# A mixture-of-experts block with attention on one core: both shared pieces of an expert period ahead of the down projection, rows turned between them, down weights split in mid-period

## What is computed

```python
x = x + 0.5 * ffn(layernorm(x));  x = x + attention(layernorm(x));  x = x + 0.5 * ffn(layernorm(x))

def ffn(inp):                                  # 4096 tokens x 256
    x = w_norm * inp * rsqrt(mean(inp**2) + 1e-6)
    w_topk, sel = top_k(softmax(x @ w_router), 4)          # 32 experts, 4 of them for a token
    buf[e] = the first 128 tokens that chose expert e      # capacity 128
    y[e] = (silu(buf[e] @ w_gate[e]) * (buf[e] @ w_up[e])) @ w_down[e]    # 256 -> 176 -> 256
    out[token] += y[e, slot] * w_topk                      # scatter-add
    shared = (silu(x @ sw_gate) * (x @ sw_up)) @ sw_down   # 256 -> 704 -> 256, for all tokens
    return inp + out + sigmoid(x @ w_shared_gate) * shared
```

## Time and profile before

| | |
|---|---|
| three runs, median (lowest to highest) | 946.34 us (943.54 to 947.62) |
| the profiled execution, its own time | 943.53 us |
| its span, first to last instruction | 941.8 us |
| TensorE busy | 899.0 us, 95% |
| VectorE busy | 731.3 us, 78% |
| ScalarE busy | 579.3 us, 62% |
| GpSimd busy | 513.9 us, 55% |
| TensorE's granted clock, mean | 0.997 |

### The profile page before, as it was taken

One profiled execution on the slowest core, in us unless ns is written; L12 is line 12 of the kernel. 1 busy time (PEld: TensorE's weight loads), 2 busy tenths in 40 slices (PEclk: granted clock), 3 DMA queues, 4 the chain that ended last, 5 costly groups with the idle time before them and its releaser, 6 DMA issues.

```text
span 941.8 us, 18520 instructions
## 1 busy us (share of the span) xinstructions
PE 899.0 (95%) x6246; PEld 688.6 (73%) x6246; DVE 731.3 (78%) x1768; ACT 579.3 (62%) x922; POOL 513.9 (55%) x537
## 2 busy tenths in 40 slices
PE   8999998999999999999999999989999989999997
PEld 6778886877878856666666666558788868778786
DVE  6998786765565889999998999988887867665545
ACT  6676744344444478878887888867667433444432
POOL 6343304456653588887887788934333045566530
PEclk9999999999999999999999999999999999999999
DMA  8143245777874610010001002004432457778735
GB/s 259 50 139 103 75 132 149 176 174 183 192 166 101 201 46 24 23 43 24 23 23 45 22 11 82 21 12 129 142 98 74 127 155 175 174 178 199 162 39 177
DMA packets 95515, 101.93 MB, mean 108 GB/s; under 512 B 18768, under 2 KB 86736, under 8 KB 95440
## 3 DMA queue, kind: packets, MB, share of 16 engines
q1 hardware_dynamic: 83152, 83.17, 29.3%
q0 software_dynamic: 12288, 17.83, 11.1%
HBM read 65.44 MB, written 35.54 MB: 107 GB/s over the span
## 4 chain that ended last, share of the span: by engine, by line
PE 52%; DVE 21%; issue 13%; POOL 6%; ACT 5%; DMA 2%; DVEq 0%; POOLq 0%; ACTq 0%
PE gu L91 6%; PE gu L93 6%; PE gu L92 6%; PE zT L1058 4%; PE pj_at L91 3%; PE pv_at L1815 3%; PE pj_at L93 3%; PE pj_at L92 3%; PE down L91 2%; PE down L93 2%; PE down L92 2%; PE scores_at L1799 2%; POOL out L841 2%; DVE turned_at L2057 2%; POOL rows L833 2%
## 5 line engine op out<-in xcount | busy, mean ns | idle before, releaser
L1144 ACT CAST a_hi<-act_gu 128x512 fp32r<-128x512 f32 x96 | 59.3, 618 | 94.6 <-DVE act_gu L1396 68.2
L91 PE MATMUL gu<-x_hi,gu_hi 128*128 128x512 f32 x264 | 113.4, 429 | 1.3 <-DVE act_gu L1396 1.2
L833 POOL DMA_INDIRECT rows<-z_rows,slots x64 | 71.1, 1110 | 67.5 <-DVE slots L1383 48.5
L1917 ACT ACTIVATE capped_at<-scores_at 128x2048 f32<-128x2048 f32 x64 | 93.1, 1454 | 20.6 <-PE scores_at L1799 20.4
L93 PE MATMUL gu<-x_lo,gu_hi 128*128 128x512 f32 x264 | 103.9, 393 | 0.0
L92 PE MATMUL gu<-x_hi,gu_lo 128*128 128x512 f32 x264 | 103.3, 391 | 0.0
L1925 ACT ACTIVATE probs_at<-capped_at 128x2048 f32<-128x2048 f32 x64 | 95.2, 1487 | 2.5
L1994 POOL TENSOR_SCALAR_AFFINE_SELECT probs_at<-probs_at 128x1024 f32<-128x1024 f32 x64 | 85.6, 1342 | 9.6 <-ACT probs_at L1925 8.8
L91 PE MATMUL down<-down_hi,a_hi 128*128 128x256 f32 x300 | 89.8, 299 | 0.6 <-DVE a_lo L1406 0.4
L1058 PE MATMUL zT<-w_gu,xT 128*128 128x352 f32 x256 | 88.4, 468 | 0.1
L841 POOL DMA_INDIRECT acc<-base,slots x32 | 51.2, 1599 | 65.2 <-DMA acc<-base,slots 53.3
(11 more groups left out here) (269 smaller groups left out, 2807.4 us busy)
## 6 DMA issues: line engine op xcount, KB each, us to landing
w_gu<-in_w_gate SPq DMA_DIRECT2D x64, 176.0 KB
w_gu<-in_w_up SPq DMA_DIRECT2D x64, 176.0 KB
w_down<-in_w_down SPq DMA_DIRECT2D x64, 176.0 KB
z_rows<-z SPq DMA_DIRECT2D x16, 512.0 KB, 3.6
acc<-base SPq DMA_DIRECT2D x10, 512.0 KB, 3.4
out<-base SPq DMA_DIRECT2D x10, 512.0 KB, 3.2
xn_at<-acc SPq DMA_DIRECT2D x16, 256.0 KB, 2.8
x<-xn_at SPq DMA_DIRECT2D x16, 256.0 KB, 2.1
```

Of the source, the lines that this page charges most:

```text
L91: nc.tensor.matmul(out, w_hi, x_hi, start=first, stop=False)
L833: pool.indirect_dma_start(out=gathered_rows[:, n, :], out_offset=None, in_=m.z_rows, in_offset=bass.IndirectOffsetOnAxis(ap=slots[:, e:e + ...
L1144: nc.scalar.copy(a_hi[rows_, mt, :], act_gu[rows_, mt % 2, :]).then_inc(a_hi_ready, 1)
L1917: nc.scalar.activation(capped[:, u % 2, :, 0:n], scores[:, :, 0:n], ACT.Tanh, scale=QK_SCALE / SOFTCAP).then_inc(capped_ready, 1)
```

## The change

Three tables of order are rewritten for the period, one for each of PE, ACT and DVE. On PE the first piece now stands directly behind `gate_up_expert`, then `turn_rows`, then the second piece, then `down_expert` and `turn_products`; only an odd period's third piece is left behind them. On ACT and DVE the split of the down weights (`high_down`, `low_down`) moves from behind the products to a place between the followups of the first and the second piece, and the second followup moves ahead of `scale` and `high_products` (ACT) and of `low_products` (DVE).

```diff
@@ on_tensor, the loop over e
                 gate_up_expert(e)
+                first_piece, second_piece, *third_piece = pieces_beside(e)
+                piece(first_piece)
                 if e + 1 < E:
                     turn_rows(e + 1)
-                first_piece, *later_pieces = pieces_beside(e)
-                piece(first_piece)
+                piece(second_piece)
                 if e > 1:
                     down_expert(e - 1)
                 turn_products(e)
-                for p in later_pieces:
+                for p in third_piece:
                     piece(p)
@@ on_scalar
                 silu_expert(e)
-                first_piece, *later_pieces = pieces_beside(e)
+                first_piece, second_piece, *third_piece = pieces_beside(e)
                 followup(first_piece)
+                high_down(e)
+                followup(second_piece)
                 if e > 1:
                     scale(e - 1)
                 high_products(e)
-                high_down(e)
-                for p in later_pieces:
+                for p in third_piece:
                     followup(p)
@@ on_vector
                 followup(first_piece)
+                low_down(e)
+                followup(second_piece)
                 low_products(e)
                 if lists:
                     list_tokens(2 + e // 2)
-                low_down(e)
-                for p in later_pieces:
+                for p in third_piece:
                     followup(p)
```

## The result

The changed kernel takes **960.63 us** (median of 4 runs, 957.59 to 961.27) where the kernel before took 944.94 beside it (4 runs, 942.54 to 947.62): ratio **1.0159**, 95% interval 1.0121 to 1.0197, so slower, by 15.7 us, some 1.6%. The forecast was 953, with a range of 945 to 959: the sign was right, the size too small. The profiled execution took 961.27 us with a span of 959.5, against 941.8 before, so 17.7 us are to be found.

The account below looks back on a forecast made before the run. It took POOL's chain of adds to bound the first stage and PE's own time the second. First stage +6.9 and second +2.0 made +8.9 on 943.53, 952.4 us, given as 953 for the median, range 945 to 959.

Parts of the forecast that it names:

- Period 0: Loop start: down_expert(0) waits for low_products, starts at 153.34 and not 152.33, +1.0 us; PE stands 2.8 us.
- Periods 1 to 3: PE stands 1.3 us at turn_rows(4) and 2.0 at the pair; expert 4 begins 2.0 us later, period 0 included.
- Add 3: POOL's chain of adds: +3.0 us at add 3, +5.4 with two clock falls of 1.2 each in periods 0 to 3.
- Periods 4 to 28: PE, each loop: shorter waits on xT outweigh new waits of turn_rows for low_products, -3.0 us.
- Its pace over 28 adds was steady at 4.59: POOL's adds 3 to 31 run at their own 4.59 us an expert, whatever PE does.
- The tail, +1.5: First stage's end: PE stands 1.04 + 3.4 us for the late rows, and a clock fall behind that costs 1.5.
- the first stage's +6.9: First stage's sum: adds +3.0, two clock falls 2.4, making +5.4 at 307.74, and a tail fall 1.5.
- Second stage, +2.0: Second loop: PE's -0.4 us plus 2.4 for two clock falls; late adds make nothing wait.
- The fall of period 30: Second stage: the clock fall behind PE's 1.51 us stand, 902.60 to 906.10, stays as before.
- rival (3): Adds 8 us behind PE hold up gathers, turn_rows waits in the second loop: 4 us more, 957; chance 0.09.
- Rival 1, the clock holds, 949: Everything as forecast without clock falls: +3.0 - 0.4 = +2.6, 949 us on the median; chance 0.25.
- It is the order around it on ACT and DVE that does: The moved split of down weights costs PE nothing by itself; the order around it on ACT and DVE does.

Follow-up runs that it names:

- e7: Changed kernel with unread matmuls filling PE's stands in periods 0 to 3, both stages: 952.64 us, ratio 1.0103.
- e9: Changed kernel with unread matmuls in all of PE's longer stands (first periods, tail, periods 17 and 30, turn_rows(31)): 949.84 us, ratio 1.0045.
- e10: Kernel before, with the changed order only in second-stage periods 4 to 28 (ACT, DVE not in 12, 24) and silu_expert(30) early: 941.36 us, ratio 0.9967.
- e11: Changed kernel without the loads of gate and up weights of experts 4 to 31: 951.84 us, ratio 1.0063.
- e12: Kernel before with 10 unread matmuls ahead of down_expert(0) in both stages: 943.47 us, ratio 0.9979.
- e8: Changed kernel with 50 unread matmuls in PE's stand in the first stage's tail: 955.5 us, ratio 1.0141.
- e14: Changed kernel with an intended move of the attention's statistics that left the instruction order the same, so a repeat: 957.88 us, ratio 1.0121.
- e1: Kernel before with only PE in the changed order, ACT and DVE in the order of before: 957.6 us, ratio 1.0140.
- e6: Kernel before without the adds of the odd experts: 943.13 us, ratio 0.9979.

## Why the prediction was right in sign and wrong in size

- **Period 0**: `down_expert(0)` at 153.34 by the count, at 153.43 in the trace, behind a stand of 2.62 us by the bracket, for the 2.8 forecast. Right.
- **Periods 1 to 3**: stands of 1.3 and 2.0 forecast, 0.82 and 1.86 in the brackets; expert 4 later by 2.0 forecast, by 2.2 with the clock held (e7). Right in the sum, the first stand forecast 0.5 too long. The two falls per loop came where they were put, and expert 4 was 3.9 late in the first loop and 4.7 in the second, against 2.0 + 2.4.
- **Add 3**: +5.4 forecast with the falls, +6.0 measured; +3.0 without, +3.5 in e7 and e9. Right.
- **Periods 4 to 28**: -3.0 forecast. From expert 5 to expert 29 PE gained 2.6 us on before in the first loop, in e9's second loop 2.3 from expert 4 on. In the second loop of the changed kernel 1.7 by expert 25, then the gathers took it back. Of the new waits of `turn_rows`, those in periods 13 and 25 came, 0.7 us each for the 0.85 forecast.
- **"Its pace over 28 adds was steady at 4.59"**: this step failed first. The chain was taken as a clock of its own, so that +5.4 at add 3 stays +5.4. It was +8.3 at add 31, at 4.67 us a step, and in e10 +1.5 became +6.1 with PE's order unchanged. An add's landing depends on what SP's loads, which follow PE, do beside it (without the gate and up loads the steps fell from 4.80 to 4.32 and +4.4 at add 3 became +1.6, e11). A mean over 28 steps looked like a constant; the single steps of the trace of before go from 4.05 to 6.77. Of the 2.9 us missed here 0.6 are add 3's; the other 2.3 an execution of the order of before can show too (2.0 in e12), so they can't all be charged to the change.
- **The tail, +1.5**: the fall itself came near that: from DVE's rows to the second loop the changed kernel loses 2.1 us, though its fall lasts 10.2 us and not 3.5 like that of 902.6, and e8, with the stand filled, loses 0.5. What failed is the stretch ahead of it, which the sum put at nothing: it let the rows come as late as the adds, +5.4 at 307.74, and they came 1.8 us later than add 31 did (10.1 against 8.3), 1.4 of it because the last add landed in 5.2 us and not 3.8. That isn't shown to be the change's doing: in e14, the same order, it landed in 4.0. So of the 5.3 us that the first stage's +6.9 lacks against 12.2, 2.9 are add 31, 1.8 the way from there to the rows, 0.6 the fall.
- **Second stage, +2.0**: 5.5 measured. The falls and expert 4 were right; what failed was to keep the gathers apart as a rival of 0.09. They are a consequence of the term that had been forecast: if the adds lag by 5 us and more, the gather behind them lags too. The second loop's adds began 18.4 us late at add 3 and were 24.4 late at add 25, behind which the gather for expert 31 is issued, while PE was 16.2 late, so 8.2 apart, the 8 that rival (3) had named; `turn_rows` stood 0.75 us for gathered rows at 907.56 and 1.13 at 912.72. The fall of period 30, which the sum kept, did not come.
- **Rival 1, the clock holds, 949**: this case was then made, by e9, and came out at 949.84. That they meet is in part luck: the rival was 2.6 us over a median of 946.34, e9 is 4.9 over one of 944.95. The first stage costs 5.2 us there, the second -0.6 (the count had +3.0 and -0.4).
- **"It is the order around it on ACT and DVE that does"** cost: too simple, by e1. Each half of the change loses alone, PE's half the more; the moved followups are what keeps the second piece's pair from waiting longer still.

What stays open is why a given add lands late in one execution and not in another, beyond the loads beside it, and whether the later statistics gain time.

## What to carry to other kernels

Count an order's own waits by hand: up to expert 4 that part came out within half a microsecond. Then ask of every late step which in-order chain hangs on it (here adds, gathers, the next stage's rows) and carry the delay through to its end, where it can have grown (from 1.5 us to 6.1 in e10) or shrunk (from 4.4 to 1.6 in e11); a mean step of such a chain is no constant. And look at each new stand of the matrix engine as a possible fall of its clock: here the same order cost 15.7 us with the falls and 4.9 with the stands filled by matmuls that nobody reads.

## What the runs showed of the hardware that was not expected

- **A stand of 1.2 us can bring the clock down or not.** The stand ahead of `down_expert(0)` in the order of before left it at 1.00 in the profiled execution of before, and was followed by a fall of 3.4 us in e10, and in e6 in both loops. The executions of the kernel before sort by their mean granted clock: of the 25 beside e9 to e11, the eleven at 0.997 and more took 941.9 to 944.0 us, the eight at 0.995 took 944.8 to 948.0, the six at 0.992 to 0.994 949.2 to 950.9. A longer stand can leave it up as well: the second-longest of the changed kernel's second loop was followed by no fall.

```profile
920.70 0.39 PE L950 MATMUL down<-down_hi,a_hi 128*128 128x256 f32 x1 [2.27 <-DVE a_hi L1411]
```

- **An add lands slower beside loads.** Over 1,008 steps of the adds in 18 traces, sorted by how long the hardware queue's packets kept the DMA engines busy in the 3 us from 1 us behind the add's start: 4.2 us a step at under 0.2 us, 4.6 at 0.8 to 1.4, 5.0 at 1.4 to 2.
- **The last add's landing has two lengths.** It took 3.8 us in before (301.09 to the loads of the attention's rows at 304.91) and 5.2 in the changed kernel, though no loads run then. In the changed kernel a transfer of the instruction queue lies beside it (packets, MB, share of 16 engines, in the 5.2 us):

```profile
q0 software_dynamic: 144, 0.13, 23.3%
q8 instruction: 1, 0.02, 1.2%
```

and in before none does (in the 3.8 us):

```profile
q0 software_dynamic: 144, 0.13, 31.0%
```

In the 18 traces with all adds, the six whose last add of the first stage took 4.4 us or more have such a transfer ending 3.2 to 4.2 us behind the add's start, and no other has one there (e8 has one that ends at 4.3, with a landing of 3.8, e14 one at 2.9, with 4.0). That goes together in every trace, but the bounds were chosen by looking and no run here made one without the other, so it isn't shown to be the cause.
